# GNN kernel: the program's branch seven groups sooner, four PSUM banks for the first sum's counts, keys decoded in parts, and the weight bounds beside chunk 0's dense layers

## The reference, cut to what matters

```python
def sage(h, src, dst):                       # four times in all
    agg = segment_sum(h[src], dst, n)        # sum over the edges that end in a node
    return agg / max(deg, 1)

h = relu(layernorm(x))
h1 = relu(concat[h, sage(h)] @ W1 + b1)                    # phase 1, 128 -> 256
x1 = x + log_softmax(concat[h1, sage(h1)] @ W2 + b2)       # phase 2, 256 -> 128
h = relu(layernorm(x1))
h2 = relu(sage(h) @ Wl0.T + bl0 + h @ Wr0.T)               # phase 3
h3 = relu(sage(h2) @ Wl1.T + bl1 + h2 @ Wr1.T)             # phase 4
out = x1 + relu(h3 @ Wa.T + ba) @ Wb.T + bb
```

## Time and profile before

| | |
|---|---|
| median of three runs | 577.35 us |
| the profiled execution | 577.56 us, its span 575.8 us |
| PE busy | 533.0 us (93%), 2918 matmuls |
| DVE busy | 232.8 us (40%) |
| ACT busy | 195.0 us (34%) |
| mean granted clock of PE | 0.993 |

### The profile page before, as it was taken

How to read it: one execution, slowest core, us unless ns; L and a number is a source line. 1 busy time by engine, 2 the same in 40 slices (tenths; PEclk the granted TensorE clock), 3 DMA queues, 4 the chain that set the end, 5 groups by cost and what they waited for, 6 DMA issues and landing times.

```text
span 575.8 us, 8914 instructions
## 1 busy us (share of the span) xinstructions
PE 533.0 (93%) x2918; PEld 278.2 (48%) x2918; DVE 232.8 (40%) x513; ACT 195.0 (34%) x352; POOL 25.8 (4%) x37
## 2 busy tenths in 40 slices
PE   1468989999999999999999999999999999999996
PEld 0254555455544554445444445544545454454555
DVE  6898996587875306667521111110000001010001
ACT  1788866567663213535521112101000010100011
POOL 4321000000000000010100000000000000000000
PEclk9997999999999999999999999999999999999999
DMA  3802232120312234344346555521110112111011
GB/s 91 203 12 63 59 108 67 56 71 21 82 35 67 78 92 127 95 114 116 84 120 170 162 151 135 144 78 36 36 54 10 45 37 53 36 36 53 18 32 30
DMA packets 72888, 44.29 MB, mean 77 GB/s; under 512 B 36059, under 2 KB 72390, under 8 KB 72726
## 3 DMA queue, kind: packets, MB, share of 16 engines
q1 hardware_dynamic: 71132, 42.66, 28.1%
q10 hardware_dynamic: 1561, 0.84, 0.6%
q0 software_dynamic: 160, 0.33, 0.2%
HBM read 19.68 MB, written 16.79 MB: 63 GB/s over the span
## 4 chain that ended last, share of the span: by engine, by line
PE 81%; DVE 8%; DMA 4%; issue 2%; SPq 2%; ACT 2%; DVEq 0%; ACTq 0%
PE ps L1251 53%; PE ps L1268 19%; PE ps L1205 6%; DVE hs_b L596 3%; SPq L357 2%; PE ps L1539 2%; DMA hs_b<-z_d 1%; DMA z_d<-zT 1%; DMA hs_b<-self_d 1%; DVE adj L625 1%; ACT adj L1021 1%; PE ps L1468 1%; DMA adj<-in_dst_dram 1%; DVE zT L754 0%; DVE adj L1648 0%
## 5 line engine op out<-in xcount | busy, mean ns | idle before, releaser
L1251 PE MATMUL ps<-adj,hs_b 125*128 (+2 forms) x1050 | 203.6, 351 | 0.0
L1251 PE MATMUL ps<-adj,hs_a 125*128 125x500 f16 (+2 forms) x700 | 158.5, 354 | 0.1
L1251 PEld LDWEIGHTS ps<-adj,hs_b 125*128 125x128 f16 x1050 | 96.3, 97 | 103.9 <-issue 6.6
L596 DVE TENSOR_TENSOR hs_b<-iota,hs_b 128x1024 f16<-128x1024 f16 x150 | 96.4, 688 | 25.0 <-PE ps L1205 24.4
L1205 PE MATMUL ps<-hs_b 128*128 128x125 f16 x625 | 68.9, 233 | 20.7 <-DVE hs_b L596 14.5
L1021 ACT ACTIVATE adj<-ps 125x500 f32 (+2 forms) x150 | 80.2, 542 | 20.9 <-PE ps L1205 14.9
L1205 PEld LDWEIGHTS ps<-hs_b 128*128 128x128 f16 x625 | 46.4, 104 | 69.1 <-DVE hs_b L596 41.1
L1251 PEld LDWEIGHTS ps<-adj,hs_a 125*128 125x128 f16 x700 | 58.9, 98 | 40.1 <-issue 5.0
L1190 ACT ACTIVATE actT<-ps,col 128x500 f32<-128x500 f32 (+1 forms) x14 | 8.9, 633 | 148.0 <-PE ps L1268 148.0
L970 DVE TENSOR_TENSOR hs_a<-ps,hs_a 125x512 f32<-125x512 f32 (+1 forms) x7 | 4.4, 635 | 128.1 <-PE ps L1539 128.1
L1268 PE MATMUL ps<-aggT,wts 128*128 128x500 f32 (+1 forms) x112 | 44.5, 539 | 0.0
(11 more groups left out here) (158 smaller groups left out, 320.0 us busy)
## 6 DMA issues: line engine op xcount, KB each, us to landing
invc<-inv_d SPq DMA_DIRECT2D x24, 250.0 KB, 3.5
h_d<-actT SPq DMA_DIRECT2D x6, 500.0 KB, 3.3
wts<-h_d SPq DMA_DIRECT2D x6, 500.0 KB, 4.0
hs_d<-hs_a SPq DMA_DIRECT2D x5, 312.5 KB
z_d<-zT SPq DMA_DIRECT2D x6, 256.0 KB, 2.1
self_d<-hs_b SPq DMA_DIRECT2D x6, 250.0 KB, 2.1
hs_b<-self_d SPq DMA_DIRECT2D x6, 250.0 KB, 3.9
hs_b<-in_x_dram SPq DMA_DIRECT2D x6, 250.0 KB
```

The lines of the kernel that those rows point to most:

```text
L596: last = nc.vector.tensor_tensor(onehots[slot], iota2.unsqueeze(1).to_broadcast(shape), keys[:, ds(g * 4, 4), :].unsqueeze(2).to_broadcast ...
L1251: last = nc.tensor.matmul(acc[:, 0:n], hs[:, ds(s * (2 * w) + part * w + h * 128, 128)], adj[0:P, ds(c * (S * C) + s * n, n)], start=(isin ...
```

## The change

- **Branch.** PE and ACT branch after group 17 rather than after group 24. Groups 18 to 24 (`counts(18, S-1)`, the last `count`, `pair(9)` to `pair(11)` and the last eviction) now stand behind it. DVE's and SP's branches stay.
- **Fill order.** PE makes counts 0 to 7 before it turns the other keys. DVE takes the second half of the moments in two parts, and decodes in parts: windows up to 256 in the fill, the rest in `second1`, between groups 6 and 7 of chunk 2. The turning of weights on PE is spread otherwise.
- **Banks.** The counts of chunk 1 rotate through banks 0, 1, 3 and 7 (`FIRST`); count i waits for the eviction of count i-4.
- **Chunk 0's dense layers.** `bounds_z` moves behind `hidden1(0)` and three more pieces; `weights_dve(0)` and `(1)` move behind `agg_out(0)` on DVE. Weight blocks 1 and 2 are turned after `second1` of chunk 1, and evicted by ACT at the end of its step for chunk 2.
- **Seams.** `own1` of the last chunk goes to bank 1 and waits for no z; loops over c on SP and ACT are written out; the store of the turned weights moves to the step c = 2; `turn2` stands at tile 17 of phase 3's lead rather than 14.

```diff
+FIRST = (0, 1, 3, 7)
...
             def step1(c):
                 next_inv(c, True)
-                if isinstance(c, int) and c == 0:
-                    store_weights()
-                else:
+                if c > 0:
                     sp.wait_ge(sem("p1_h0T"), c + 1)
                     turn_own(1, c + 1, hs_d1, turned1)
+                    if c == 2:
+                        store_weights()
                     self_rows(c - 1, True)
                     z_rows(c - 1)
...
-                step1(0)
-                with sp.Fori(1, NFULL - 1) as c:
+                for c in range(NFULL - 1):
                     step1(c)
...
-                build_c(2, True, 0, 2)
+                build_c(2, True, 0, 1)
+                split(2 * QW, NPAD)
+                dve.wait_ge(sem("split"), 8)
+                build_c(2, True, 1, 2)
                 degrees_of_windows()
-                build_c(2, True, 2, 3)
-                weights_dve(dve, 0)
+                build_c(2, True, 2, 4)
                 own_sum(1, 0, turned1)
-                build_c(2, True, 3, 4)
-                weights_dve(dve, 1)
+                build_c(2, True, 4, 5)
                 dve.wait_ge(sem("inv_out"), 16)
                 nc.vector.memset(zboth.rearrange("p (t n) -> p t n", n=PT)[:, :, P:PT], 0.0)
                 agg_out(0, True)
-                build_c(2, True, 4, 7)
+                build_c(2, True, 5, 6)
+                weights_dve(dve, 0)
+                build_c(2, True, 6, 7)
+                weights_dve(dve, 1)
                 own_sum(1, 1, turned1)
...
         def act_layers(act, slow):
+
+            pair(act, 9)
+            norm(act, 14, 15)
+            pair(act, 10)
+            pair(act, 11)
+            act.wait_ge(sem("counted"), S)
+            nc.scalar.activation(columns(0, True, (S - 1) * (C // S), C // S), bank(7, C, P).rearrange("p (d t) -> p t d", t=S),
+                                 ACT.Copy).then_inc(sem("evicted"), 1)
...
-                build(2, True, 6, 12)
-                build(2, True, 13, 13)
-                turned_out(act, 1, 5)
-                build(2, True, 14, 14)
-                turned_out(act, 2, 6)
-                build(2, True, 14, 18)
+                build(2, True, 6, 18)
...
                 second1()
+                step1(2, True, True)
+                turned_out(act, 1, 4)
+                turned_out(act, 2, 5)
+                step1(3, True, True)
                 act.wait_ge(sem("wt_out"), 16)
-                with act.Fori(2, NFULL - 1) as c:
+                for c in range(4, NFULL - 1):
                     step1(c, True, True)
...
         def pe_layers(pe, slow):
+            counts(18, S - 1)
+            count(S - 1, S - 1, True, 0, b=7)
...
-                    pe.wait_ge(sem("p1_zlo"), NFULL)
-                own(ha, D, 0, 6, c, full).then_inc(sem("p1_own"), 1)
+                own(ha, D, 0, 6 if slow else 1, c, full).then_inc(sem("p1_own"), 1)
...
-                    count(S + i, i, True, S + i - 1)
+                    count(S + i, i, True, S + i - 3, b=FIRST[i % 4])
...
-                    pieces(10, 14)
-                    bounds_z(pe)
+                    pieces(10, 19)
                     pe.wait_ge(sem("wt"), 3)
-                    turn_weights(1, 5)
-                    turn_weights(2, 6)
-                    pieces(14, 19)
-                    pe.wait_ge(sem("wt"), 5)
                     pe.wait_ge(sem("absw"), 2)
                     hidden1(c - 1, True)
-                    pieces(19, S).then_inc(sem("p1_agg"), 1)
+                    pieces(19, 22)
+                    bounds_z(pe)
+                    pieces(22, S).then_inc(sem("p1_agg"), 1)
...
                 second1(c - 1, True)
+                if c == 2:
+                    turn_weights(1, 4)
+                    turn_weights(2, 5)
...
-                   [(14, turn2, NFULL)], ((0, "p2_low", NFULL - 1), (20, "p2_low", NFULL), (24, "p2_low", NCH)), fill={20: 5, 24: 8})
+                   [(17, turn2, NFULL)], ((0, "p2_low", NFULL - 1), (20, "p2_low", NFULL), (24, "p2_low", NCH)), fill={20: 5, 24: 8})
...
             dve.wait_ge(sem("k_int"), 1)
-            split(lk, 0, QW)
+            split_n(lk, 0, QW)
+            split(0, QW)
             dve.wait_ge(sem("split"), 2)
             dve.wait_ge(sem("ident"), 3)
-            for i in range(8):
+            for i in range(9):
                 onehot(i)
+            stats(lk, XA, 15)
+            for i in range(9, 11):
+                onehot(i)
+            stats(lk, 15, MOMENTS[1][1])
+            onehot(11)
+            moments(lk, *MOMENTS[1])
+            onehot(12)
             dve.wait_ge(sem("k_int"), 2)
-            split(lk, QW, NPAD)
+            split_n(lk, QW, NPAD)
+            split(QW, 2 * QW)
+            onehot(13)
...
-            counts(0, 4)
+            counts(0, 8)
...
-            counts(4, 13)
+            counts(8, 14)
...
-            counts(13, 15)
             pe.wait_ge(sem("w_in"), 16 * NW)
-            pe.wait_ge(sem("k_int"), 2)
             turn_weights(0, 4)
-            counts(15, 18)
+            counts(14, 16)
             turn_weights(3, 5)
-            counts(18, 21)
+            counts(16, 18)
+            pe.wait_ge(sem("k_int"), 2)
             turn_weights(4, 6)
-            counts(21, S - 1)
             pe.wait_ge(sem("flag"), 1)
-            count(S - 1, S - 1, True, 0, b=7)
             branch(pe, pe_layers)
```

91 lines of the change are left out of this document (42 added, 49 removed).

## The result

| | before | changed |
|---|---|---|
| median beside each other | 576.89 us (4 runs) | 571.72 us (4 runs, 570.36 to 572.56) |
| ratio, 95% interval | | 0.990 (0.988 to 0.992) |
| the same pair, measured once more | 577.48 us (11 runs) | 572.85 us (5 runs), 0.992 (0.991 to 0.993) |
| the profiled execution | 577.56, span 575.8 | 572.56, span 570.8 |
| PE, DVE, ACT busy | 533.0, 232.8, 195.0 | 533.3, 232.8, 193.5 |

What follows compares the result with a forecast made beforehand. It took the first 218 us as deciding, bound by the order of nearly full PE, DVE and ACT. Terms -0.9, -1.3, -2.6, +0.7, -0.1 sum to -4.2 us: 573.4 profiled, 573.2 median, range 570.9 to 575.6.

Steps and rivals of the forecast that it cites:

- fill, to the sum's first product: End of the fill: first sum starts at 43.6 in place of 44.48, -0.9 us; bounds -1.9 to +0.8.
- first sum: First sum: four banks remove most ACT waits, one stays near piece 14, slow pieces stay; -1.3 us, bounds -2.2 and -0.4.
- chunk 1, to hidden1(0): Chunk 1's sum: one-hot waits, turned blocks and bounds_z leave; hidden1(0), held by agg_out and inverse degrees, moves by 3.3 us.
- from there to second1(0): Behind hidden1(0): bounds_z comes back (0.4) and second1 waits for the bounds' second stage (0.3); 0.7 us lost.
- chunks 2 and 3, to chunk 4's first count: Chunks 2 and 3: turned blocks +0.1, ACT's scaled evictions at the seam +0.3, weights' store +0.3; +0.7 us.
- seam to phase 2: own1 of the last chunk: its 1.31 us wait moves to turn1 and the next turn; -0.1 us.
- a wait of over 1 us for z in chunk 3: Chunk 3: one of the listed signs that would show the forecast wrong.
- I price that at 1.4 us (its row): Fill: cost of ACT's flag load inside its own chain once moved seven groups earlier; bounds 0.55 and 2.0 us.
- Cheap load: Rival, fill and first sum: PE and ACT pay what DVE pays, clock up from the start; -5.8 us, 571.6; chance 0.13.
- I price that at +0.3: Chunks 2 and 3: cost of the 1152 KB weights' store going out ahead of z's store; bounds 0 and +2.1 us.
- SP's queue: Rival: z's store waits for the weights, z lands 2.1 us late, +1.8 more; gain 2.4, 575.0; chance 0.14.
- DVE is the bound: Rival, early branch to chunk 1's end: DVE has no idle time left; +1.8 us slower, 579.2; chance 0.06.

Runs made afterwards that it cites:

- c4_quiet: Changed kernel with PE's and ACT's branches behind group 24 and h0's first row store held behind ACT's first eviction of the first sum; 572.86 us, 0.9918.
- a2_banks: Changed kernel with the first sum's counts in two banks again, count i waiting for the eviction of count i-2; 574.07 us, 0.9934 of the kernel before.
- a3_bounds: Changed kernel with bounds_z and weights_dve(0) and (1) back in their old places ahead of agg_out(0); 576.34 us, 0.9977 of the kernel before.

## Why the prediction was right, point by point

Leads against the kernel before, at the same landmarks of the two profiles:

| term | predicted | measured in the trace |
|---|---|---|
| fill, to the sum's first product | -0.9 | -1.69 (44.48 to 42.79) |
| first sum | -1.3 | -1.27 |
| chunk 1, to hidden1(0) | -3.3 | -3.50 |
| from there to second1(0) | +0.7 | +0.43 |
| chunks 2 and 3, to chunk 4's first count | +0.7 | +1.21 |
| chunks 4 and 5 | 0 | +0.45 |
| seam to phase 2 | -0.1 | -0.47 |
| behind it | 0 | -0.2 |
| sum | -4.2 | -5.0 |

The sign, the order of the terms and the range held. Two terms were mis-sized, the fill by 0.8 us too little gain and the store by 0.8 too little loss. They cancel, so a part of the closeness of 573.2 to 571.7 and 572.9 is luck. One of the signs of being wrong came true as well, "a wait of over 1 us for z in chunk 3": it is 1.03.

*The load.* The step that failed is "I price that at 1.4 us (its row)". The row was read rightly, but it was a price at 42 us, beside the first store of rows; c4_quiet shows that without the store the load costs 0.48. Moved seven groups ahead it meets no store. The other half of the term was right: ACT's last eviction ends at 42.65 in place of 43.22, so with 0.48 for the load the wait that I took as gone, 1.0, came to 1.05. I had this as the rival Cheap load, but tied it to a clock that would stay up, and gave it 0.13; its load came true and its clock did not. Its bound for the term, -1.9, is close to the -1.69 that came. The Trainium skill's floor of about 600 ns (DMA: Bandwidth & Descriptors, Latency and other measured facts) is nearer to all short loads here (0.48 to 0.55 on PE, ACT and DVE, 0.67 on SP) than my price was, though the loads of PE, ACT and DVE lie below it, so it is no floor here; and "some 0.8 us better" by it is what the term gained over its forecast.

*The store of the weights.* The step that failed is "I price that at +0.3". It was 1.1 at the place, the added 1.5 us in z's landing less PE's slack, within the bounds of 0 to 2.1. I had put 14% on the rival *SP's queue*, which priced the collision at 2.1. The other two parts of that term, the turned blocks and ACT's seam, came to 0.1 rather than 0.4. The two stores were issued 4.0 us apart and z landed 1.5 us late. The Trainium skill (DMA: Bandwidth & Descriptors, Two DMAs through the same engine are not ordered) says that within one queue of an engine descriptors start in order. The direction agrees with it, but the data do not tell a queue that starts in order from engines that are merely shared.

*Right by its own steps.* The first sum: the one wait left is that near piece 14 (0.81 us at 55.41), and the slow pieces are as many as before. The profile names a one-hot for it, but DVE itself stands for PE's count right behind it (0.61 us up to 55.98), so DVE was ahead; ACT's first eviction behind the second high parts starts at 54.69, as forecast. a2_banks gives the same 1.2 to 1.3 from the other side. That the term came to within 0.03 is partly luck: in the second profile of the changed kernel, with a low clock half as long, the stretch is 19.60 us, and the term would be -2.07. Chunk 1: hidden1 follows agg_out, and agg_out waits for the inverse degrees, as foreseen; DVE had the room that the rival "DVE is the bound" denied. Its own place in the argument is in a3_bounds, where DVE really is the bound. The second stage of the bounds was in time for second1, so +0.43 (bounds_z alone) came in place of +0.7. The seam: own1's wait turned into one of 0.72 at turn1 and 0.32 at turn2, as forecast; that the lead grew there by 0.47 is more than the -0.1, within what this stretch varies by between kernels that don't differ in it.

*Not foreseen.* The +0.45 of chunks 4 and 5 comes through z as well: during chunk 4's sum its four turning reads take 5.79 us, before 4.96, and PE waits 0.33 us at 157.87.

## What to carry to other kernels

The price of a register load is that of its neighbourhood: before moving one, look at which DMA runs beside it, and price it at both places. When an order is mended so that a wait goes, look at the granted clock behind the next gap of PE: with products that nobody reads in the gaps of the fill, the slow pieces of the next stretch went. Profile a kernel twice before a difference of 1 us in one stretch is put down to an edit: the two profiles of the changed kernel differ by as much. And a bulk store with no deadline belongs behind the small store that someone waits for, on the same queue; that was one line here.
